# Windowed attention with a linear layer: scores of the next window ahead of time, or in their own window with the output projection behind them

## What is computed

```python
q = x @ Wq + bq;  k = x @ Wk + bk;  v = x @ Wv + bv      # heads of 64
dots = einsum('bwie,bwje->bwij', bq, bk) * d ** (-0.5)   # 128 queries x 256 keys
dots = where(causal_mask | pad_mask, mask_value, dots)
out = einsum('bwij,bwje->bwie', softmax(dots), bv)
x = layernorm(x + out @ Wo + bo)
x = layernorm(x + (x @ W.T + b) + (x @ V_r) @ C.T)
```

## Time and profile before

| | us |
|---|---|
| time of each run | 2840.05, 2940.26 |
| median | 2890.15 |
| the profiled execution's own time | 2839.18 |
| its span on the slowest core (core 4) | 2837.6 |
| spans of the eight cores | 2831.0 to 2837.6 |
| mean granted clock of TensorE, as a share of full speed | 0.793 to 0.795 |
| PE busy with matmuls | 1800.7 (63%) |
| ACT busy | 855.1 (30%) |
| DVE busy | 842.1 (30%) |
| POOL busy | 414.0 (15%) |

### The profile page before, as it was taken

The page is one execution under the profiler, slowest core; times in us unless marked ns, Lnnn a source line. Parts: engine busy times, 40 slices in busy tenths (PEclk is TensorE's granted clock), DMA queues, the critical chain, the costliest instruction groups (busy, mean ns, idle before and its releaser), DMA issues.

```text
span 2837.6 us, 37519 instructions; the slowest of 8 cores (2831.0 to 2837.6 us)
## 1 busy us (share of the span) xinstructions
PE 1800.7 (63%) x12734; PEld 919.4 (32%) x12924; DVE 842.1 (30%) x1966; ACT 855.1 (30%) x1381; POOL 414.0 (15%) x297
## 2 busy tenths in 40 slices
PE   0136775858577575857667585756758585675855
PEld 0013332424333333423333243333324233333422
DVE  1112323333232333233232233323233332323322
ACT  1202233332323323232432323242232323233232
POOL 0010111120211111021111102121110212111011
PEclk9967786968788696978878697877869787786966
DMA  6420100111110011111001111101011111100000
GB/s 186 114 74 16 45 14 25 45 30 38 31 45 15 24 45 31 38 31 45 17 29 40 28 38 30 45 27 38 23 28 38 30 45 28 48 13 26 8 23 23
DMA packets 111296, 107.62 MB, mean 38 GB/s; under 512 B 89602, under 2 KB 89602, under 8 KB 111108
## 3 DMA queue, kind: packets, MB, share of 16 engines
q1 hardware_dynamic: 101892, 71.66, 8.8%
q0 software_dynamic: 9216, 33.56, 3.0%
HBM read 54.81 MB, written 33.55 MB: 31 GB/s over the span
## 4 chain that ended last, share of the span: by engine, by line
PE 54%; ACT 16%; DVE 15%; issue 7%; DMA 4%; SPq 2%; DVEq 1%; ACTq 1%; POOL 0%; POOLq 0%
PE p L685 14%; PE p L394 12%; PE p L488 10%; ACT ep L773 9%; PE p L708 8%; DVE ep L622 4%; PE u L836 4%; DVE y L454 3%; ACT aofm L544 3%; ACT outb L581 2%; PE u L377 2%; DVE y L514 2%; DVE x2fm L414 2%; DVE aofm L383 2%; PE u L408 1%
## 5 line engine op out<-in xcount | busy, mean ns | idle before, releaser
L773 ACT ACTIVATE ep<-ps 128x512 bf16<-128x512 f32 x496 | 296.1, 597 | 733.8 <-PE ps L752 667.5
L394 PE MATMUL p<-wo,aofm 128*128 128x512 bf16 x961 | 328.5, 513 | 79.4 <-DVE aofm L383 78.6
L622 DVE TENSOR_TENSOR ep<-ep,m 128x1536 bf16<-128x1536 bf16 (+1 forms) x128 | 126.8, 991 | 757.4 <-ACT ep L773 736.1
L526 POOL DMA_DIRECT2D out<-outb x64 | 36.7, 573 | 2127.2 <-ACT outb L581 1692.0
L488 PE MATMUL p<-wt,x2fm 128*128 128x512 bf16 x961 | 282.5, 458 | 13.8 <-issue 13.5
L752 PE MATMUL ps<-qfm,kfm 64*128 64x128 bf16 x1792 | 131.3, 236 | 248.4 <-ACT ep L773 245.4
L685 PE MATMUL p<-xfm,wq 128*128 128x512 bf16 x1007 | 226.8, 381 | 59.7 <-DMA xfm<-xb 38.6
L718 ACT CAST v_sb<-p 128x512 bf16<-128x512 f32 x128 | 74.9, 585 | 623.2 <-PE p L708 623.2
L644 PE MATMUL u<-ones_c,ep 128*128 128x1 bf16 x2016 | 70.3, 164 | 296.3 <-DVE ep L622 296.1
L544 ACT ACTIVATE aofm<-y 128x1024 bf16<-128x1024 f32 x128 | 135.2, 1056 | 385.5 <-DVE y L454 211.2
L708 PE MATMUL p<-wv,xfm 128*128 128x512 bf16 x1008 | 222.8, 379 | 0.8
(11 more groups left out here) (81 smaller groups left out, 1780.5 us busy)
## 6 DMA issues: line engine op xcount, KB each, us to landing
x_sb<-x SPq DMA_DIRECT2D x16, 2048.0 KB, 9.5
out<-outb POOLq DMA_DIRECT2D x64, 512.0 KB, 3.0
xfm<-xb SPq DMA_TRANSPOSE x512, 2.3
y<-Wq SPq DMA_DIRECT2D x8, 512.0 KB, 4.7
y<-Wk SPq DMA_DIRECT2D x8, 512.0 KB, 4.2
y<-Wv SPq DMA_DIRECT2D x8, 512.0 KB, 4.3
y<-Wo SPq DMA_DIRECT2D x8, 512.0 KB, 4.2
y<-Wf SPq DMA_DIRECT2D x8, 512.0 KB, 4.2
```

The source lines that it names most:

```text
L394: fns = [(lambda e, ci=ci, b=bank, h=half: e.matmul(b[:], aofm[:, ci, :], wo[:, ci, h * 512:(h + 1) * 512], start=(ci == 0), stop=(ci == N ...
L622: tok = kb.emit("ve", lambda e, v=view, n=n: e.tensor_tensor(out=v, in0=v, in1=m01[:].unsqueeze(1).broadcast_to([128, n, 128]), op=ALU.mul ...
L773: tok = kb.emit("ac", lambda e, b=bank, g=g: e.activation(ep[:, g, :], b[:], AF.Exp, scale=0.125), waits=bres.rd() + eres.wr(), inc="ac")
```

## The change

The scores are no longer done ahead. In each pass all eight groups are done in their own window, then XR, then A2, then one mask over all 16 diagonal pieces, then all sums. A1 moves to the start of the pass, ahead of X, and X uses bank u0 in place of u1, so that the two sets of transposes need not wait for each other's bank. The projections go round four banks, p0, p1, ps2 and ps3, in place of two. Nothing is computed in another way.

```diff
@@ the bank of X
-            u1bf = u1[:].bitcast(BF16)
+            u0bf = u0[:].bitcast(BF16)
@@ the start of a pass
             if gi - 1 >= 0 and gi - 1 < NW and PHASE >= 4:
+                post_A1(gi - 1)
                 pre_B(gi - 1)
             if gi - 2 >= 0 and PHASE >= 4:
                 post_X(gi - 2)
@@ the banks of the projections
+                qkv_banks = [(p0, R["p0"]), (p1, R["p1"]),
+                             (ps[2], R["s2"]), (ps[3], R["s3"])]
...
-                        bank = p0 if co % 2 == 0 else p1
-                        bres = R["p0"] if co % 2 == 0 else R["p1"]
+                        bank, bres = qkv_banks[co % 4]
...
-                        bank = p0 if (tc % 2) == 0 else p1
-                        bres = R["p0"] if (tc % 2) == 0 else R["p1"]
+                        bank, bres = qkv_banks[(half * STW + tc) % 4]
@@ scores and what follows them
-            if att and wt_ == 0 and PHASE >= 2:
-                scores_half(gi, 0, 6)
-            if gi - 1 >= 0 and gi - 1 < NW and PHASE >= 4:
-                post_A1(gi - 1)
+            for g in (range(8) if att and PHASE >= 2 else []):
...
+            if gi - 2 >= 0 and PHASE >= 4:
+                post_XR(gi - 2)
             if gi - 1 >= 0 and gi - 1 < NW and PHASE >= 4:
                 post_A2(gi - 1)
-            if att and PHASE >= 2:
-                scores_half(gi, 6, 8)
 
             if att and PHASE >= 3 and SUB >= 2:
-                if wt_ == 0:
-                    mask_part(gi, 0, 6)
-                mask_part(gi, 6, 8)
-
-            if gi - 2 >= 0 and PHASE >= 4:
-                post_XR(gi - 2)
+                ep_cur = ep[:].rearrange("p g (hhjt x) -> p (g hhjt) x",
+                                         x=128)[:, 1::2, :]
...
+                    in1=m01[:].unsqueeze(1).broadcast_to([128, 16, 128]),
@@ the end of a pass
-            if PHASE >= 2 and gi + 1 < NW and (gi + 1) % STW != 0:
-                scores_half(gi + 1, 0, 6)
-                if PHASE >= 3 and SUB >= 2:
-                    mask_part(gi + 1, 0, 6)
-                if PHASE >= 3:
-                    sums_part(gi + 1, 0, 6)
```

More of the change, by code:

```diff
@@ L408, in post_X @@
             fns = [(lambda e, c=c, pw=pw: e.transpose(
-                u1bf[0:128, c * 128:(c + 1) * 128],
+                u0bf[0:128, c * 128:(c + 1) * 128],
                 x2b[:, pw, c * 128:(c + 1) * 128], ident[:])) for c in range(NCH)]
-            tok = kb.group("pe", fns, waits=x2b_r.rd() + R["u1"].wr(), inc="pe")
+            tok = kb.group("pe", fns, waits=x2b_r.rd() + R["u0"].wr(), inc="pe")
             x2b_r.did_rd(tok)
-            R["u1"].did_wr(tok)
+            R["u0"].did_wr(tok)
             tok = kb.emit("ve", lambda e, pw=pw: e.tensor_copy(
-                out=x2fm[:, pw], in_=u1bf[0:128, 0:1024].rearrange(
+                out=x2fm[:, pw], in_=u0bf[0:128, 0:1024].rearrange(
                     "p (c f) -> p c f", c=NCH)),
-                waits=R["u1"].rd() + x2fm_r.wr(), inc="ve")
-            R["u1"].did_rd(tok)
+                waits=R["u0"].rd() + x2fm_r.wr(), inc="ve")
+            R["u0"].did_rd(tok)
             x2fm_r.did_wr(tok)
@@ new lines, in build_program @@
+            if att and PHASE >= 3:
+                fns = []
+                sum_waits = R["u0"].wr() + R["ones"].rd()
+                for h in range(H):
+                    g, hh = h % 8, h // 8
+                    jts = [1] if first else [0, 1]
+                    for jt in jts:
+                        reg = (2 * hh + jt) * 128
+                        st_ = (len(jts) == 1) or (jt == jts[0])
+                        sp_ = (len(jts) == 1) or (jt == jts[-1])
+                        fns.append(lambda e, g=g, r=reg, h=h, st=st_, sp=sp_:
+                                   e.matmul(u0[:, h:h + 1], ep[:, g, r:r + 128],
+                                            ones_c[:], start=st, stop=sp))
+                for g in range(8):
+                    sum_waits += R[f"ep{g}"].rd()
+                tok = kb.group("pe", fns, waits=sum_waits, inc="pe")
+                R["u0"].did_wr(tok)
+                for g in range(8):
+                    R[f"ep{g}"].did_rd(tok)
```

138 lines of the change are left out of this document (52 added, 86 removed).

## The result

The changed kernel is faster by a good deal more than was forecast. Its median is 2363.82 us of nine runs, against 2840.1 us of eight runs of the kernel before, and the ratio is 0.8326 (95% interval 0.8315 to 0.8336). Some executions of either kernel are several per cent longer with a lower granted clock on one die (2573.22 us is such a one); ratios and windows here leave them out. The profiled execution took 2362.8 us with a span of 2361.2 us on core 2. Against the execution that the prediction worked from, the span is 476.4 us shorter.

The account below looks back on a forecast made before the run. PE's work and its waits, chiefly for the mask, were taken to bound the kernel. Short windows save 7.6 x 47 = 357 us, projection windows 1.5 x 15 = 23: 2839 - 380 = 2459 us, range 2370 to 2600.

Parts of the forecast that it names:

- The mechanism: Short windows: A2 covers the mask, removing the sums' 296.1 us of waits except what projection windows keep; 7.6 us saved each.
- The tail from the sums' end to C1's end: Reciprocal, residual adds, correction, attention times V and C1 in short windows: unchanged, taken as 9.0 us, bounds 8.5 to 10.2.
- The claim of the data side: Casts and transposes for the next block: nothing moved nearer its limit, about 20 us left over in three short windows.
- the length of A2: Output projection on PE behind XR in short windows: kept at 6.0 us, bounds 3.6 to 6.8.
- a clock that stays up: Rival: PE keeps 2.4 GHz through XR and A2, short window 22.4 us, total 2313 us; chance 0.08.
- The base: Short window of the kernel before, C1's end to C1's end, read from one block of four windows: 33.1 us.
- a 47th window: Of 48 windows without projections, 47 were counted because window 1 has no C1 ahead; each saves 7.6 us.
- the projection window: Window with projections, 15 times behind a C1: 62.6 us against 64.1, saving 1.5 each, 23 us in all.
- The mask of 2048: Single mask operation behind the eighth exponential: 2.1 us, not below 1.56, covered by A2 in short windows.
- Dense stretches below full clock: Rival: projections lose a tenth of the clock, 2533 us, or drop to 13/16 of it, 2613; throttling's chance 0.06.
- The slower side: Rival: projections run at 1.2 GHz, up to 41.7 us more a block, at most 3126 us; chance 0.02.
- the rival below: The rival of PE keeping 2.4 GHz through XR and A2: 146 us less than forecast, 2313 us; chance 0.08.

Follow-up runs that it names:

- b_no_ahead: Kernel before, with scores of groups 0 to 5, their mask and sums done in their own window instead of ahead: 2511.4 us, ratio 0.8839.
- a_a2_late: Changed kernel with A2 moved from behind XR to behind the sums: 2433.5 us, ratio 0.8491.
- a_two_banks: Changed kernel with the projections back in two banks, p0 and p1: 2402.7 us, ratio 0.8377.
- b_fill: Kernel before, with 18 idle matmuls in PE's wait for the mask, ahead of the sums of groups 0 to 5: 2796.2 us, ratio 0.9842.
- a_gap: Changed kernel with A2 also made to wait for the eighth exponential: 2435.5 us, ratio 0.8572.
- a_split: Changed kernel with scores 6 and 7 put behind A2 again: 2646.8 us, ratio 0.9325.
- a_fill: Changed kernel with 18 idle matmuls between scores 3 and 4 of the short windows, in the LayerNorm stall: 2351.1 us, ratio 0.8203.
- a_x_u1: Changed kernel with X back in bank u1 in every window, still behind A1: 2486.5 us, ratio 0.8693.
- a_fill_all: Changed kernel with idle matmuls in short windows: 18 ahead of score 4, two ahead of each of 5 to 7; also six ahead of the correction: 2204.8 us, ratio 0.7772.

## Why the prediction was right and wrong

**The mechanism was right.** The forecast said that the wait of the sums for the mask goes because A2 comes between them; it went from 296.1 to 3.1 us. b_no_ahead, which only takes away the work ahead of time, has 69% of the gain, and a_a2_late brings the wait back with A2 moved away. The two sets of transposes fell into the LayerNorm stall and their waits went. XR started 8.65 us behind C1 in the mean of the 46 short windows, for 8.6 forecast, bound by the exponential. The wait at the correction stayed at 112.7. The tail from the sums' end to C1's end was 8.75 us, for 9.0. The wait of the projections for qfm is gone, and a_two_banks prices it at 27 us. The claim of the data side held: no wait for `xfm` appeared beyond the one at the start.

**The step that failed is the length of A2.** The forecast kept 6.0 us for the short windows, on the ground that the stall ahead of it is as long. From A2's start to the start of the sums it measured 4.6 us in the mean (in the kernel before 5.9), 1.4 less than the forecast, 63 us over 46 windows. The reason given for it was the wrong one to lean on: the stall's length does not fix A2's clock. What precedes A2 in the changed kernel is not only the stall but 3.2 us of scores and 1.0 of XR with pauses of 0.16 us, and in the kernel before it was two sets of transposes with a pause of 0.94 ahead of A1 and of A2. In b_fill, with a busy PE in the stall, A2 took 3.6; in a_gap, with a pause of 1.22 ahead of it, 5.3; in a_split, with two scores fewer and a pause of 1.65 ahead of XR, it was 0.5 longer. All three fit that the denser work made it shorter, but a_fill filled the far end of the stall and gained next to nothing, and the projection windows of b_fill show the same steps with A2 at 3.6 and at 6.1. So that A2's length follows PE's activity is shown, and why it came to 4.6 and not another value stays open. Half of the rival "a clock that stays up" was therefore true, in A2 alone: XR ran at the low level (1.01 us, for 0.62 before), and C1 rose from 307.4 to 333.8 us.

**The base was read from one block.** The prediction took 33.1 us as the short window of before; the mean over the trace is 33.5, 17 us over 46 windows.

**How the 97 us between 477 and 380 are made up.** Behind C1 the mean short window of the changed kernel has the start of A2 at 9.6 us, of the sums at 14.2, their end at 15.15 and C1's end at 23.9, where the forecast had 9.4, 15.4, 16.5 and 25.5. That is 1.6 us, 74 us over 46 windows: A2's 63 and 11 of smaller terms. The base adds 17. The start up to the first C1 and the last two windows gave 16, and the forecast had 8 for a 47th window in their place. The windows with projections gave 21, 2 less than forecast.

**Luck in the projection window.** It saved 1.4 us, for 1.5 forecast, but by errors that cancelled. A2 was put at 3.5 us there, at full clock, and took 4.6 from its start to the sums', and the tail behind the sums was put at 10.2 and took 8.8. The mask, put 0.4 us late, was not late.

**Terms that were off and hidden.** The mask of 2048 was put at 2.1 us and took 1.375 in the mean, 1.23 with POOL idle, below the 1.56 that was called its floor: the 1557 ns of the shorter form were a mean of two kinds. In the kernel before and in b_no_ahead it takes 0.96 us while POOL is idle and mostly 1.86 beside POOL's addition L499. It ran under A2 in any case. The price of the bank of X was not in the forecast at all; with A1 ahead of the projections it is what keeps 5 us off every block (a_x_u1).

**The rivals.** Dense stretches below full clock did not come: a matmul of the projections takes 380 ns in the mean in both kernels (core 3). The Trainium skill's rule of 13/16 ("TensorE: Matmul & The Clock Gate", section "Seeing it yourself") does not show in the traces of before and after, nor in a_fill_all with its mean granted clock of 0.967. Its level does show elsewhere: in a_a2_late the granted clock of core 7 is 0.81 from 1291 to 1296 us, in the projections, and cores 4 to 7 of a_a2_late, a_x_u1 and a_fill had 9 to 15 such stretches each, none over 6.5 us, while cores 0 to 3 beside them had none. None of them lasted through the 41.7 us of projections. The slower side did not come near. The range was too narrow on its low side: the bounds of A2 (3.6 to 6.8) were named, but only half of the rival below was let in, and the base's own spread was left out.

## What to carry to other kernels

An in-order engine pays for work put ahead of time if that work itself waits for another engine; the same steps behind a long independent piece (here 16 matmuls) cost nothing here. When a step is moved, look at the two places where it now stands in front of something, and at every window type: X behind A1 in one bank cost 0.7 us in one kind of window and 5 us in the other. On a TensorE whose clock moves with its work, do not carry the length of a stretch over from a stall of equal length: give it the bounds of both clock levels, and price two slow stretches together, since speeding one can slow the other. Read the base over all windows and not over one block.
